# Moving the last maxima, a norm and a projection within the passes of a fused attention and expert block

## The chip, the core and the metric

The kernel runs on one core of a Trainium2 chip. The metric is the device time of one execution in microseconds, the median of several. Times of single instructions come from one profiled execution. TensorE has two clock levels, 1.2 and 2.4 GHz; "granted clock" is the mean level of a stretch as a share of the higher one.

## The reference

The input x has 64 sequences of 128 tokens with 128 features, the context 64 sequences of 120 tokens with 96 features. Both attentions have 16 heads of 8 features.

```
x = x + tanh(g_xattn) * cross_attention(layernorm(x), ctx, Wq.. bo)
x = x + tanh(g_ffn) * ffn(layernorm(x), ...)

ffn(x):
  h = rms(x, n1_w); q, k = rms per head of h@wq.T, h@wk.T; v = h@wv.T
  x = x + causal_attention(q, k, v) @ wo.T          (first 32 columns of it set to 0)
  xf = rms(x, n2_w)
  wts = top 2 of 4 of softmax(xf @ gate_w.T), normalised
  moe = wts0 * gelu(xf@e0_up)@e0_down + wts1 * (silu(xf@e1_w1) * (xf@e1_w2))@e1_down
      + wts2 * gelu(gelu(gelu(xf@e2_l1)@e2_l2)@e2_l3)@e2_l4
      + wts3 * gelu(gelu(xf@e3_down)@e3_up)@e3_out
  return x + moe                                    (first 32 columns of moe set to 0)
```

The layer norm of the second block and the rms norm inside it are nested: with v the variance and r = (v + 1e-5)^-1/2, h is (x - mean) * r * (r * r * v + 1.19e-7)^-1/2.

## The kernel before

**Groups and parts.** The 64 sequences go in 16 groups of 4. Five parts work on a group one after the other: N (layer norm, transposes, q, k and v of cross-attention), A (cross-attention), B (inputs of self-attention), D (self-attention, expert inputs and gates), M (the rest of the experts and the store). They are pipelined over groups: in step t, N works on group t + 1, A on t, B on t - 1, D on t - 2, M on t - 3. Steps -1 to 2 are the ramp, with fewer parts, steps 3 to 14 are a hardware loop of twelve passes, steps 15 to 18 the tail.

**Order.** Nothing is scheduled automatically. `SCHEDULE` is a list of works written by hand (`self_attention`, `second_experts`, `cross_attention`, `first_experts`), and every engine walks through the same list and issues its share of each work, in order. Ramp and tail steps take either the works of their parts from `SCHEDULE` or a list of their own (`second_group`, `third_group`, `last_self_values`). Engines wait for each other by semaphores: `filled` and `drained` of each PSUM bank, and named ones.

**Banks.** A work that writes PSUM takes the next bank of its ring: "w" has four (w0 to w3), "s2" and "f" are two names of the two banks s2a and s2b, "pv" and "t" have one each. PE may fill a bank when its previous use is drained.

**The scores of a sequence.** `estimate` computes rough scores of one sequence, in four works "s1", one per four heads, all issued together in four w banks (a quad). DVE takes their negative row maxima into mpad (L888, four TENSOR_REDUCE of 128x512 or 128x480). When the fourth sequence is done, "mT" transposes mpad on PE (L1098), ACT copies it to mT (L747), and SP issues four small DMAs that write it as extra rows into the stack of queries qd (L528, the semaphore m_loaded). `exact` computes the exact scores with these rows (L1110), which begin with waits for m_loaded and stacks_loaded; ACT takes their exponentials into probs (L766), POOL masks the causal ones. `values` multiplies by V, which ACT copies from the work "v". "oT", "nT" and "wo" normalise and project pairs of sequences.

**Nested norms.** After the second "wo" of A, DVE computes the statistics of x1 (L782 to L790). POOL makes, in six operations with two powers, the factors rB (L630 to L640): rB[0] is r for x2, rB[5] is the product for the input of self-attention. "A norm" on DVE applies the latter and writes hb; "hT" transposes hb on PE at the start of the next pass.

**Others.** "N stats" and "N norm" are the layer norm of the next group: DVE, one power on POOL (rsA, L608), and DVE again (xn, L819). "D out" writes yb, "D squares" is a square on POOL, a sum and a tiny operation on DVE, and leads to the power rM on POOL for "D norm". "gates 0" to "gates 3" are thirteen tiny DVE operations in four pieces. `queries_or_keys` copies q or k twice on ACT (L694, L699), `low_part` makes the remainder on DVE (L797, split_q and split_k) and drains the bank, `block_diagonal_keys` makes kd (L805).

## Time and profile before

| | us |
|---|---|
| median of 3 runs | 1191.6 |
| lowest and highest | 1188.81, 1195.52 |
| profiled execution, device time | 1192.36 |
| profiled execution, span of the core | 1190.6 |

| engine | busy us | share |
|---|---|---|
| PE (TensorE, matmuls) | 1038.0 | 87% |
| DVE (VectorE) | 792.6 | 67% |
| ACT (ScalarE) | 735.7 | 62% |
| POOL (GpSimd) | 351.5 | 30% |

The mean granted clock of TensorE is 0.941. A timeline row gives the start in us, the duration, the engine, the line, the operation, what it writes and reads, the shapes and the count, and in brackets the idle time ahead of it with what ended that idleness. Rows of one line merge several instructions. A group of the page gives busy time and mean ns, and after the bar the idle time before and what ended most of it.

### The profile page before, as it was taken

The page shows a single profiled execution, that of the slowest core. Times are in us where ns is not written, and L with a number is a line of the kernel's source. Part 1 is how long each engine was busy: PE and PEld are TensorE (multiplying, and loading weights), DVE is VectorE, ACT ScalarE, POOL GpSimd, SP SyncE. Part 2 cuts the span into 40 slices and gives each one's busy share as a digit, 9 for nine tenths or more (in the row PEclk, how much of TensorE's full clock was granted, in tenths as well). Part 3 has the DMA queues.
Part 4 walks back from the last instruction along what each step waited for, and adds up shares of the span by engine and source line. Part 5 has one row for each costly group of instructions (what it writes and reads, how often), then busy time and mean ns, then how long its engine had stood idle before and what let it go on. Part 6 is the DMA issues. An engine that isn't in the chain of part 4 may idle for free.

```text
span 1190.6 us, 26283 instructions
## 1 busy us (share of the span) xinstructions
PE 1038.0 (87%) x8578; PEld 645.1 (54%) x8578; DVE 792.6 (67%) x2153; ACT 735.7 (62%) x1329; POOL 351.5 (30%) x522
## 2 busy tenths in 40 slices
PE   3647798999999998999999999999999898988797
PEld 1324455555555565555565665555565555555454
DVE  7266666767777767777767676767767676764523
ACT  1334566767576666767666766767666676756353
POOL 4611415133141414133141514224141513214030
PEclk8667789999999999999999999999999999999899
DMA  5144444433434444333344444334344443220300
GB/s 179 32 119 107 120 108 120 110 101 90 103 67 115 119 116 119 90 99 99 93 88 115 119 116 106 90 100 98 79 114 115 119 114 98 82 45 34 83 1 18
DMA packets 78693, 114.27 MB, mean 96 GB/s; under 512 B 9153, under 2 KB 41537, under 8 KB 78529
## 3 DMA queue, kind: packets, MB, share of 16 engines
q1 hardware_dynamic: 78368, 111.58, 37.2%
q10 hardware_dynamic: 288, 2.21, 0.5%
q8 instruction: 22, 0.36, 0.1%
q14 instruction: 15, 0.11, 0.0%
HBM read 58.97 MB, written 53.74 MB: 95 GB/s over the span
## 4 chain that ended last, share of the span: by engine, by line
PE 55%; issue 17%; DVE 15%; ACT 6%; POOL 3%; DMA 2%; SPq 2%; DVEq 0%; POOLq 0%; ACTq 0%
PE ps_w L1157 11%; PE ps_pv L1131 7%; PE ps_s2a L1110 7%; PE ps_s2b L1110 5%; DVE mpadB L888 4%; PE ps_w L1175 4%; PE ps_t L1016 3%; PE ps_w L1016 3%; PE ps_w L1060 3%; DMA qdB<-mTB 2%; SPq L528 2%; PE ps_w L1092 2%; ACT probs L766 2%; DVE mpadA L888 2%; PE ps_w L1030 2%
## 5 line engine op out<-in xcount | busy, mean ns | idle before, releaser
L766 ACT ACTIVATE probs<-ps_s2a 120x512 f32<-120x512 f32 (+1 forms) x256 | 152.9, 597 | 129.7 <-PE ps_s2a L1110 124.6
L888 DVE TENSOR_REDUCE mpadA<-ps_w 128x4 f32<-128x480 f32 x256 | 150.3, 652 | 50.6 <-PE ps_w L1092 50.6
L888 DVE TENSOR_REDUCE mpadB<-ps_w 128x4 f32<-128x512 f32 x256 | 158.8, 685 | 28.9 <-PE ps_w L1092 28.9
L1157 PE MATMUL ps_w<-W,hid 128*128 128x96 f32 x1024 | 142.4, 298 | 18.6 <-DVE split_q L797 16.0
L1157 PEld LDWEIGHTS ps_w<-W,hid 128*128 128x128 f32 x1024 | 134.9, 212 | 33.8 <-DVE split_q L797 20.8
L766 ACT ACTIVATE probs<-ps_s2b 120x512 f32<-120x512 f32 (+1 forms) x256 | 152.6, 596 | 0.2 <-PE ps_s2b L1110 0.2
L666 POOL TENSOR_SCALAR_AFFINE_SELECT probs<-probs 128x1024 f32<-128x1024 f32 x128 | 140.0, 1093 | 0.0
L630 POOL TENSOR_TENSOR rB<-veB,neg_half 128x4 f32<-128x4 f32 x16 | 16.1, 1008 | 394.4 <-DVE veB L790 394.4
L1110 PE MATMUL ps_s2a<-qdB,kstB 128*128 128x512 f32 x128 | 66.1, 517 | 38.9 <-DMA qdB<-mTB 32.5
L1175 PE MATMUL ps_w<-xfT,W 128*128 128x512 f32 x160 | 85.0, 620 | 0.0
L665 POOL TENSOR_TENSOR tick<-one 128x1 f32<-128x1 f32 x128 | 24.9, 195 | 186.9 <-ACT probs L766 183.1
L1168 PE MATMUL ps_s2a<-hid,W 128*128 128x512 f32 x160 | 79.2, 609 | 0.0
L917 DVE SCALAR_TENSOR_TENSOR ym<-ps_w,gates,ym 128x96 f32<-128x96 f32 x192 | 47.6, 311 | 47.1 <-PE ps_w L1157 47.1
L762 ACT ACTIVATE hid<-ps_s2a 128x512 f32<-128x512 f32 x80 | 47.8, 598 | 47.2 <-PE ps_s2a L1168 34.6
L1110 PE MATMUL ps_s2a<-qdA,kstA 128*120 128x512 f32 x128 | 65.5, 511 | 10.9 <-DMA qdA<-mTA 4.7
L770 ACT ACTIVATE oT<-ps_pv 128x512 f32<-128x512 f32 x64 | 38.2, 598 | 51.8 <-PE ps_pv L1131 51.5
L1131 PE MATMUL ps_pv<-probs,VA 120*18 120x128 f32 x2048 | 70.0, 278 | 0.0
L1131 PE MATMUL ps_pv<-probs,VB 128*18 128x128 f32 x2048 | 68.7, 274 | 0.1
L617 POOL TENSOR_TENSOR xf<-x 128x512 f32<-128x512 f32 x16 | 16.6, 1040 | 170.4 <-DVE yb L949 170.4
L1131 PEld LDWEIGHTS ps_pv<-probs,VA 120*18 120x18 f32 x2048 | 51.3, 99 | 24.1 <-issue 23.4
L1110 PEld LDWEIGHTS ps_s2a<-qdB,kstB 128*128 128x128 f32 x128 | 24.8, 194 | 70.3 <-issue 56.8
L1131 PEld LDWEIGHTS ps_pv<-probs,VB 128*18 128x18 f32 x2048 | 50.4, 97 | 18.5 <-issue 17.7
(176 smaller groups left out, 2096.3 us busy)
## 6 DMA issues: line engine op xcount, KB each, us to landing
scratch_Aq<-split_q SPq DMA_DIRECT2D x48, 256.0 KB, 2.4
qdA<-scratch_Aq SPq DMA_DIRECT2D x64, 192.0 KB
scratch_Bq<-split_q SPq DMA_DIRECT2D x48, 256.0 KB, 2.4
scratch_Bk<-split_k SPq DMA_DIRECT2D x48, 256.0 KB, 3.0
qdB<-scratch_Bq SPq DMA_DIRECT2D x64, 192.0 KB
kstB<-scratch_Bk SPq DMA_DIRECT2D x64, 192.0 KB
scratch_Ak<-split_k SPq DMA_DIRECT2D x48, 240.0 KB, 2.9
kstA<-scratch_Ak SPq DMA_DIRECT2D x64, 180.0 KB
```

Of the source, the lines that this page charges most:

```text
L666: pool.affine_select(out=tile, in_=tile, compare_op=ALU.is_ge, fill=0.0, base=0, pattern=[[0, 2 * HT], [1, P]], channel_multiplier=-1).the ...
L762: nc.scalar.activation(hid[:, HID_AT[index[0]] + index[1], :], bank[:], ACT.Gelu).then_inc(done, 1)
L766: nc.scalar.activation(probs[0:k, slot_of(part, *index), :], bank[0:k, :], ACT.Exp, scale=SCALE if part == "A" else 1.0).then_inc(done, 1)
L770: nc.scalar.activation(oT[:], bank[:], ACT.Copy).then_inc(done, 1)
L888: nc.vector.tensor_reduce(mneg[OP[part]][:, :, c, b], bank[:, 0:HT * k].rearrange("p (h k) -> p h k", h=HT), AX.X, ALU.max, negate=True).t ...
L917: ins = nc.vector.scalar_tensor_tensor(out=ym[:, b, KEEP:P], in0=bank[:, b * UP:(b + 1) * UP], scalar=gates[:, b, e:e + 1], in1=y[:, b, KE ...
L1016: ins = nc.tensor.transpose(psum[st.bank[key]][:, b * P:(b + 1) * P], of(b), identf[:])
L1110: mm(o, kst[p][:, c, b * k:(b + 1) * k], qd[p][:, :, c, b * P:(b + 1) * P], start=True, stop=True).then_inc(done, 1)
L1131: ins = mm(psum[st.bank[last]][32 * j:32 * j + VS, at:at + P], VB[p][0:k, first:first + VS], probs[0:k, slot_of(part, b, c), j * P:(j + 1) ...
L1157: ins = mm(bank[:, b * UP:(b + 1) * UP], hid[:, HID_AT[h] + k, b * P:(b + 1) * P], w[f"down{index[1]}"][:, k * UP:(k + 1) * UP], start=k = ...
L1168: ins = mm(bank[:], w[name][:, k * HID + c * P:k * HID + (c + 1) * P], hid[:, HID_AT[h] + k, :], start=k == 0, stop=k == chunks[-1])
L1175: mm(bank[:], w[name][:, c * P:(c + 1) * P], xfT[:], start=True, stop=True).then_inc(done, 1)
```

## The change

Five edits, all but one moves in the lists. (1) In `first_experts`, estimate B 3 goes from behind "wo" 1 of A, its statistics and the base of the next group, to behind "nT" 1; "mT" of B goes ahead of q and v; the second pair of silu fills (e1_w1 and e1_w2, index 1) goes from ring w to ring f; gates 1 goes ahead of q, gates 2 ahead of "A norm", v and k. (2) In `second_experts`, "N norm" goes ahead of "wo" 1 and "out" of D, and "D squares" behind qT and kT. (3) In `cross_attention`, the projection v of B goes behind the first pair of exact scores. (4) The factor of the nested norms becomes one power of (v * (1 + RMS_EPS) + RMS_EPS * LN_EPS), which DVE computes as vrB beside veB; POOL has two operations instead of six, and x2's initial value now waits for b_pow. (5) In ramp and tail steps ("st.parts != PARTS") SP issues two of the four maxima DMAs and ACT the other two, and the diagonal keys of N are made ahead of the low part of k. `third_group` and `last_self_values` are changed alike.

```
-            + one("D", "out", 0, None) + one("D", "squares", 0, None) + one("N", "norm", 0, None) + one("B", "qT") + one("B", "kT")
+            + one("D", "out", 0, None) + one("B", "qT") + one("B", "kT") + one("D", "squares", 0, None)
...
-    return (one("B", "v") + exact("A", 0, 0) + down(2) + exact("A", 0, 2) + one("N", "xT")
+    return (exact("A", 0, 0) + one("B", "v") + down(2) + exact("A", 0, 2) + one("N", "xT")
...
-                        for j in range(HT):
+                        for j in range(HT if st.parts == PARTS else HT // 2):
...
+                        pool.tensor_tensor(rB[:, 1], vrB[:], neg_half[:], ALU.pow).then_inc(b_rs, 1)
                         pool.tensor_tensor(rB[:, 0], veB[:], neg_half[:], ALU.pow).then_inc(b_pow, 1)
-                        pool.wait_ge(b_pow, g * 5 + 1)
-                        pool.tensor_tensor(rB[:, 1], rB[:, 0], rB[:, 0], ALU.mult).then_inc(b_pow, 1)
-                        pool.wait_ge(b_pow, g * 5 + 2)
-                        pool.tensor_tensor(rB[:, 2], rB[:, 1], mvB[:, :, 1], ALU.mult).then_inc(b_pow, 1)
-                        pool.wait_ge(b_pow, g * 5 + 3)
-                        pool.tensor_tensor(rB[:, 3], rB[:, 2], rms_eps[:], ALU.add).then_inc(b_pow, 1)
-                        pool.wait_ge(b_pow, g * 5 + 4)
-                        pool.tensor_tensor(rB[:, 4], rB[:, 3], neg_half[:], ALU.pow).then_inc(b_pow, 1)
-                        pool.wait_ge(b_pow, g * 5 + 5)
-                        pool.tensor_tensor(rB[:, 5], rB[:, 4], rB[:, 0], ALU.mult).then_inc(b_rs, 1)
...
+                        if st.parts != PARTS:
+                            act.wait_ge(done, st.fills(*key))
+                            for j in range(HT // 2, HT):
...
+                if both is not None:
+                    nc.vector.tensor_scalar(both[:], mv[:, :, 1], 1.0 + RMS_EPS, RMS_EPS * LN_EPS, ALU.mult, ALU.add).then_inc(stats, 1)
...
+                        if work == "k" and st.parts != PARTS:
+                            block_diagonal_keys(part, "A", g)
```

The three places below are taken from step 2 of the ramp, which walks through the same list as a pass of the loop, only without part M, and so without its rows.

The first is PE's end of a step, from the second silu fill to the transpose of the maxima or the projections of the next group. Line 1175 is a fill of experts from xfT, 1016 "nT", 1088 and 1092 the estimate with the causal rows, 1144 "wo", 1030, 1040 and 1034 q, v and k, 1098 "mT". Before:

```order
L1175 MATMUL ps_w<-xfT,W 128x512
L1016 MATMUL ps_t<-identf,on 128x128 x2
L1175 MATMUL ps_s2b<-xfT,W 128x512
L1144 MATMUL ps_t<-W,onT 128x128 x2
L1088 MATMUL ps_w<-causal_k,causal_q 128x512 x4
L1092 MATMUL ps_w<-kdB,qTbB 128x512 x4
L1175 MATMUL ps_s2a<-xfT,W 128x512
L1175 MATMUL ps_s2b<-xfT,W 128x512
L1030 MATMUL ps_w<-xnT,W 128x512
L1040 MATMUL ps_w<-W,ctT 120x128 x4
L1098 MATMUL ps_w<-identf,mpadB 128x128
```

The same place in the changed kernel, whose lines are numbered five higher here:

```order
L1180 MATMUL ps_s2a<-xfT,W 128x512
L1021 MATMUL ps_t<-identf,on 128x128 x2
L1093 MATMUL ps_w<-causal_k,causal_q 128x512 x4
L1097 MATMUL ps_w<-kdB,qTbB 128x512 x4
L1180 MATMUL ps_s2b<-xfT,W 128x512
L1149 MATMUL ps_t<-W,onT 128x128 x2
L1180 MATMUL ps_s2a<-xfT,W 128x512
L1180 MATMUL ps_s2b<-xfT,W 128x512
L1103 MATMUL ps_w<-identf,mpadB 128x128
L1035 MATMUL ps_w<-xnT,W 128x512
L1045 MATMUL ps_w<-W,ctT 120x128 x4
```

The estimate has moved ahead of one fill and "wo", the transpose of the maxima ahead of q and v, and the silu fill is in an s2 bank.

The second is DVE at the same place, from x1 or the maxima on. Line 937 is x1, 782 to 790 the statistics, 888 the maxima, 797 the low part, 973 to 975 gates 1, 834 hb. Before:

```order
L937 SCALAR_TENSOR_TENSOR x<-ps_t,tg,xb 128x256
L782 BN_STATS stB<-x 128x6 x4
L785 MEMSET sm 128x1
L787 BN_AGGR mvB<-stB 128x2 x4
L790 TENSOR_SCALAR veB<-mvB 128x4
L888 TENSOR_REDUCE mpadB<-ps_w 128x4 x4
L797 SCALAR_TENSOR_TENSOR split_q<-ps_w,vc,split_q 128x512
L973 TENSOR_REDUCE sm<-lg 128x4
L974 RECIPROCAL sm<-sm 128x4
L975 TENSOR_TENSOR lg<-lg,sm 128x16
L834 TENSOR_SCALAR hb<-x,mvB,rB 128x128 x4
L797 SCALAR_TENSOR_TENSOR split_k<-ps_w,vc,split_k 128x480
```

In the changed kernel:

```order
L893 TENSOR_REDUCE mpadB<-ps_w 128x4 x4
L942 SCALAR_TENSOR_TENSOR x<-ps_t,tg,xb 128x256
L781 BN_STATS stB<-x 128x6 x4
L784 MEMSET sm 128x1
L786 BN_AGGR mvB<-stB 128x2 x4
L790 TENSOR_SCALAR vrB<-mvB 128x4
L791 TENSOR_SCALAR veB<-mvB 128x4
L978 TENSOR_REDUCE sm<-lg 128x4
L979 RECIPROCAL sm<-sm 128x4
L980 TENSOR_TENSOR lg<-lg,sm 128x16
L798 SCALAR_TENSOR_TENSOR split_q<-ps_w,vc,split_q 128x512
L984 TENSOR_TENSOR cmp<-lg 128x4x3
```

The maxima have moved ahead of x1 and the statistics, gates 1 ahead of split_q; behind the last row come seven more of gates 2 and only then hb.

The third is DVE between the statistics of the next group and the diagonal keys of B. Line 942 is "wo" 1 of D, 949 "out", 847 and 849 "squares", 819 "N norm". Before:

```order
L942 TENSOR_TENSOR x<-ps_t,x 128x2x96
L949 SCALAR_TENSOR_TENSOR yb<-x,tg,xc 128x512
L847 TENSOR_REDUCE ssM<-xf 128x4
L849 TENSOR_SCALAR msM<-ssM 128x4
L819 TENSOR_SCALAR xn<-xt,mvA,rsA 128x128 x4
L797 SCALAR_TENSOR_TENSOR split_q<-ps_w,qns,split_q 128x512
L797 SCALAR_TENSOR_TENSOR split_k<-ps_w,vc,split_k 128x512
```

In the changed kernel:

```order
L820 TENSOR_SCALAR xn<-xt,mvA,rsA 128x128 x4
L947 TENSOR_TENSOR x<-ps_t,x 128x2x96
L954 SCALAR_TENSOR_TENSOR yb<-x,tg,xc 128x512
L798 SCALAR_TENSOR_TENSOR split_q<-ps_w,qns,split_q 128x512
L798 SCALAR_TENSOR_TENSOR split_k<-ps_w,vc,split_k 128x512
L806 TENSOR_SCALAR kdB<-kTbB,pick 128x512 x4
L849 TENSOR_REDUCE ssM<-xf 128x4
L851 TENSOR_SCALAR msM<-ssM 128x4
```

The norm is now ahead of "wo" and "out", the sum of squares behind the diagonal keys.

## Rows read from the trace of the kernel before

**Rows 1.** Stretches: us, busy PE, PEld, DVE, ACT, POOL, clock, DMA share, GB/s.
```profile
526.82:593.18 66.36, 61.52 (x537) 37.98 (x537) 48.65 (x137) 45.73 (x83) 20.16 (x29) 1.00 0.42 105
593.18:661.06 67.88, 63.03 (x536) 39.67 (x537) 48.65 (x137) 45.85 (x83) 20.16 (x29) 0.97 0.41 103
593.80:597.30 3.50, 3.50 (x19) 3.50 (x18) 0.83 (x5) 1.68 (x3) 1.60 (x3) 0.53 0.94 340
626.00:628.00 2.00, 0.71 (x7) 0.67 (x7) 2.00 (x6) 1.97 (x3) 1.51 (x2) 1.00 0.00 0
```

**Rows 2.** The page's costliest groups: down projection; first bank of exact scores.
```profile
L1157 PE MATMUL ps_w<-W,hid 128*128 128x96 f32 x1024 | 142.4, 298 | 18.6 <-DVE split_q L797 16.0
...
L1110 PE MATMUL ps_s2a<-qdB,kstB 128*128 128x512 f32 x128 | 66.1, 517 | 38.9 <-DMA qdB<-mTB 32.5
```

**Rows 3.** Timeline of PE at the end of one pass and the next's start.
```profile
649.67 0.44 PE L1016 MATMUL ps_t<-identf,on 128*128 128x128 f32 x2
...
654.12 1.12 PE L1030 MATMUL ps_w<-xnT,W 128*128 128x512 f32 x2 [0.25 <-DVE mpadB L888]
...
661.06 0.49 PE L1110 MATMUL ps_s2a<-qdB,kstB 128*128 128x512 f32 x1 [2.22 <-DMA qdB<-mTB]
...
668.39 0.38 PE L1092 MATMUL ps_w<-kdA,qTbA 32*128 32x480 bf16 x4
```

**Rows 4.** Timelines of DVE, ACT and POOL over the same seam.
```profile
651.98 0.87 DVE L782 BATCH_NORM_STATS2 stB<-x 128x6 f32<-128x128 f32 x4
...
653.38 2.48 DVE L888 TENSOR_REDUCE mpadB<-ps_w 128x4 f32<-128x512 f32 x4
656.58 0.75 DVE L797 SCALAR_TENSOR_TENSOR split_q<-ps_w,vc,split_q 128x512 fp32r<-128x512 f32 x1 [0.72 <-ACT split_q L699]
...
658.08 1.12 DVE L834 TENSOR_SCALAR hb<-x,mvB,rB 128x128 f32<-128x128 f32 x4
...
660.75 0.18 DVE L979 TENSOR_TENSOR cmp<-lg 128x12 f32<-128x12 f32 x1
...
661.79 0.17 DVE L985 TENSOR_REDUCE sm<-lg 128x4 f32<-128x16 f32 x1
...
655.28 0.69 ACT L694 ACTIVATE qTbA<-ps_w,vc 128x512 bf16<-128x512 f32 x1 [0.77 <-PE ps_w L1030]
...
656.97 0.26 ACT L747 ACTIVATE mTB<-ps_w 64x128 fp32r<-64x128 f32 x1
...
659.49 1.28 ACT L766 ACT_TABLE_LOAD   x1
...
653.55 1.01 POOL L630 TENSOR_TENSOR rB<-veB,neg_half 128x4 f32<-128x4 f32 x1 [26.04 <-DVE veB L790]
...
656.74 1.27 POOL L649 TENSOR_TENSOR xb<-xt,gxbo 128x512 f32<-128x512 f32 x1
```

**Rows 5.** Timelines of PE, DVE, POOL and ACT at the start of cross-attention.
```profile
627.33 2.02 PE L1157 MATMUL ps_w<-W,hid 128*128 128x96 f32 x16 [1.29 <-DVE split_q L797]
...
625.50 1.12 DVE L819 TENSOR_SCALAR xn<-xt,mvA,rsA 128x128 f32<-128x128 f32 x4
626.53 0.75 DVE L797 SCALAR_TENSOR_TENSOR split_q<-ps_w,qns,split_q 128x512 fp32r<-128x512 f32 x1
...
624.45 1.02 POOL L608 TENSOR_TENSOR rsA<-veA,neg_half 128x4 f32<-128x4 f32 x1
...
626.30 1.28 ACT L766 ACT_TABLE_LOAD   x1
627.59 0.60 ACT L766 ACTIVATE probs<-ps_s2a 120x512 f32<-120x512 f32 x1
```

**Rows 6.** Timeline of PE in ramp steps 0 and 1 and tail step 15.
```profile
37.70 0.75 PE L1110 MATMUL ps_s2a<-qdA,kstA 128*120 128x512 f32 x1 [4.71 <-DMA qdA<-mTA]
...
125.35 0.77 PE L1110 MATMUL ps_s2a<-qdB,kstB 128*128 128x512 f32 x1 [2.81 <-issue]
...
1060.95 0.33 PE L1098 MATMUL ps_w<-identf,mpadB 128*128 128x128 f32 x1 [2.04 <-DVE mpadB L888]
```

More of the change, by code:

```diff
@@ L147, in first_experts @@
     return (fill("D", "e1_w1", 0, "w") + one("A", "wo", 0, "t") + fill("D", "e1_w2", 0, "w") + values("A", 3)
-            + one("D", "gates", 0, None) + fill("D", "e1_w1", 1, "w") + one("A", "oT", 1, "t") + fill("D", "e1_w2", 1, "w")
-            + one("A", "nT", 1, "t") + fill("D", "e2_l1", 0) + one("A", "wo", 1, "t") + one("A", "stats", 0, None)
-            + one("N", "base", 0, None) + estimate("B", 3) + fill("D", "e2_l1", 1) + fill("D", "e3_down", 0) + one("N", "q")
-            + one("D", "gates", 1, None) + one("A", "norm", 0, None) + one("N", "v") + one("B", "mT") + one("N", "k")
-            + fill("D", "e0_up", 0) + one("D", "gates", 2, None) + fill("D", "e0_up", 1, "w") + one("D", "gates", 3, None))
+            + one("D", "gates", 0, None) + fill("D", "e1_w1", 1) + one("A", "oT", 1, "t") + fill("D", "e1_w2", 1)
+            + one("A", "nT", 1, "t") + estimate("B", 3) + fill("D", "e2_l1", 0) + one("A", "wo", 1, "t") + one("A", "stats", 0, None)
+            + one("N", "base", 0, None) + fill("D", "e2_l1", 1) + fill("D", "e3_down", 0) + one("D", "gates", 1, None)
+            + one("B", "mT") + one("N", "q") + one("D", "gates", 2, None) + one("A", "norm", 0, None) + one("N", "v") + one("N", "k")
+            + fill("D", "e0_up", 0) + fill("D", "e0_up", 1, "w") + one("D", "gates", 3, None))
 def slot_of(part, b, c):
@@ L160, with of_parts @@
 SCHEDULE = self_attention() + second_experts() + cross_attention() + first_experts()
+def of_parts(parts, order=None):
+    return [use for use in order or SCHEDULE if use[0] in parts]
 def first_group():
@@ L192, in third_group @@
             + one("B", "init", 0, None) + one("B", "copy", 0, None) + values("A", 0)
-            + exact("A", 2, 0) + one("N", "xT") + exact("A", 2, 2) + values("A", 1)
-            + exact("A", 3, 0) + one("A", "oT", 0, "t") + estimate("B", 1) + exact("A", 3, 2) + values("A", 2)
-            + one("A", "nT", 0, "t") + one("A", "wo", 0, "t") + values("A", 3) + estimate("B", 2)
+            + exact("A", 2, 0) + estimate("B", 1) + exact("A", 2, 2) + one("N", "xT") + values("A", 1)
+            + exact("A", 3, 0) + one("A", "oT", 0, "t") + estimate("B", 2) + exact("A", 3, 2) + values("A", 2)
+            + one("A", "nT", 0, "t") + one("A", "wo", 0, "t") + values("A", 3) + estimate("B", 3)
             + one("A", "oT", 1, "t") + one("A", "nT", 1, "t") + one("A", "wo", 1, "t")
-            + one("A", "stats", 0, None) + one("N", "base", 0, None) + estimate("B", 3)
-            + one("N", "q") + one("A", "norm", 0, None) + one("N", "v") + one("B", "mT") + one("N", "k"))
+            + one("A", "stats", 0, None) + one("N", "base", 0, None) + one("B", "mT")
+            + one("N", "q") + one("N", "v") + one("A", "norm", 0, None) + one("N", "k"))
 def last_self_values():
@@ L210, in last_self_values @@
             + fill("D", "e1_w1", 0, "w") + fill("D", "e1_w2", 0, "w") + one("D", "gates", 0, None)
-            + fill("D", "e1_w1", 1, "w") + fill("D", "e1_w2", 1, "w") + fill("D", "e2_l1", 0) + one("D", "gates", 1, None)
+            + fill("D", "e1_w1", 1) + fill("D", "e1_w2", 1) + fill("D", "e2_l1", 0) + one("D", "gates", 1, None)
             + fill("D", "e2_l1", 1) + fill("D", "e3_down", 0) + one("D", "gates", 2, None)
@@ L245, in uses_before @@
     return n
-def of_parts(parts):
-    return [use for use in SCHEDULE if use[0] in parts]
 PARTS = "NABDM"
@@ L402, in build @@
         rsA = sb("rsA", [P, G])
-        rB = sb("rB", [P, 6, G])
+        rB = sb("rB", [P, 2, G])
+        vrB = sb("vrB", [P, G])
         hs, hr = sb("hs", [P, 2 * H * G]), sb("hr", [P, 2 * H * G])
@@ L778, in _, with statistics @@
         def _(dve):
-            def statistics(src, stats_of, mv, ve, stats, g):
+            def statistics(src, stats_of, mv, ve, stats, g, both=None):
+                n = g * (4 if both is not None else 3)
                 for b in range(G):
@@ L829, in step @@
                             dve.wait_ge(drained[b], n)
-                        statistics(x1, stB, mvB, veB, b_stats, g)
+                        statistics(x1, stB, mvB, veB, b_stats, g, both=vrB)
                     elif (part, work) == ("A", "norm"):
@@ L837, in step @@
                     elif (part, work) == ("B", "init"):
+                        dve.wait_ge(b_pow, g + 1)
                         if not st.first("B"):
```

18 lines of the change are left out of this document (11 added, 7 removed).

## The prediction

> **What bounds the kernel now.** I read the page's costliest groups first, for what TensorE (PE) waits for, then PE's timeline, then those of VectorE (DVE), ScalarE (ACT) and GpSimd (POOL) at the two waits found. PE is the bound: of a loop pass of 66.36 us it is busy for 61.52 [rows 1]. A pass is one trip of the twelve-trip loop; self-attention of group g starts each with the first exact scores of part D. Two waits stand out in the groups: 32.5 us before these first scores, for the DMA of the row maxima (qdB<-mTB), and 16.0 us before a down projection, for DVE's split_q [rows 2].
>
> The first wait is 2.22 us in the pass shown [rows 3]; 13 seams between passes (the ramp's last step ahead of them) have it alike. It costs more than its length. A pass without a fallen clock lasts 66.36 us, one with it 67.88; in the latter the granted clock is about half (0.53, so mostly 1.2 of the 2.4 GHz) for the 3.5 us right after the wait [rows 1]. I counted 11 such falls behind the 13 waits. The second wait, 1.29 us, is not followed by one: the clock across it is 1.00 [rows 1, 5]. So a fall costs 67.88 - 66.36 = 1.5 us, and only the long wait brings it.
>
> **Seam between two passes, before.** From the transposes of the second normalised pair (nT, 649.67) to the first estimate of the next pass (668.39) PE takes 18.72 us [rows 3]: 0.25 waiting for DVE's maxima before q, 2.22 for the DMA, 1.5 for the clock, the rest work. The maxima of the fourth quad start on DVE at 653.38 only, because x1 and its statistics stand ahead (from 651.98) [rows 4]. Their transpose then waits behind q and v, ACT copies it at 656.97 [rows 4], and from there to the first scores it is 661.06 - 656.97 = 4.09 us: the copy, four issues on SP's queue, the landing.
>
> **Seam, after.** PE runs nT, then the estimate. Its four banks are free by then, since the second silu pair has gone from ring w to ring f. DVE ends the silu product at about 651.0 (x1, 0.5 us, stands between it and 651.98 with 0.4 of idleness), takes the four maxima in the 2.48 us of its row, until 653.5, then x1 (0.5), statistics with one more tiny operation (1.5 + 0.17), until 655.6. PE meanwhile does e2_l1, wo, e2_l1 and e3_down: the same steps that lay between nT and q before, whose 654.12 less the 0.25 of wait is 653.87, so it reaches the maxima transpose at about 653.8, with the maxima just done. ACT has the gelu of e3_down ahead of the copy, which I place at 654.45. Plus 4.09 the maxima have landed at 658.55. PE has the same steps before it as from 654.12 to 658.84 (661.06 less 2.22), 4.7 us, and is there at about 658.5: a wait under 0.1 instead of 2.22.
>
> Behind that three things come close. (1) hb: POOL's first power takes 1.01 us [rows 4], so b_rs stands at 656.7, in place of a chain of six that took 3.2 us until the next POOL operation began. One power alone is enough to keep POOL off the path, but DVE now has gates 1 (0.8: from split_q's end, 656.58 + 0.67, to hb at 658.08) and gates 2 (660.75 to 661.79, 1.04) ahead of hb [rows 4]. Its line is split_q 656.4 to 657.1, gates 2 to 658.15, hb to 659.2; PE wants hb at 659.0. Wait 0.2. (2) The drain of k by DVE, 0.7 later, against the down projection at 659.8: 0.1. (3) ACT: from q's first copy to the end of its table load is a closed row of work, 655.28 to 660.77 before; it ends at 660.55 after, while PE comes 2.5 us earlier. Exponentials, hT, exponentials, four copies of qk then end at 664.95, and the estimate, which needs all four banks, starts at 665.05 where PE was ready at 664.7: 0.35. So the seam ends at 665.05 - 649.67 = 15.4 instead of 18.7: 3.34 saved where the clock fell, 1.84 where it did not. 13 x 1.84 + 11 x 1.5 = 40.4 us.
>
> A rule of the Trainium skill speaks against (3). ScalarE: Activation LUTs (What ACT_TABLE_LOAD costs) says that a switch costs a load of 1283 ns and a drain of about 1380 ns. The trace has the load alone: it starts at 626.30 behind a copy and takes 1.28, and the exponential follows at 627.59, 0.01 us later [rows 5]. By the page the start of D would be 1.4 us later in 13 passes, 18 us less gain; I go by the rows.
>
> **Start of cross-attention.** Before: PE does v, then the first pair of scores, until about 626.0, and waits 1.29 us until 627.33 because DVE's split_q runs at 626.53 only; ahead of it stands the norm of the next group (xn, 625.50, 1.12 us), which waits for POOL's power at 624.45, itself queued behind POOL's square of x2 [rows 5]. After: the power is first on POOL, right behind the statistics, and xn (1.12) fills a stretch in which DVE stood idle before wo; wo and out follow, and split_q comes some 1.6 us earlier, at about 624.9, so that the bank is free before PE wants it at 625.9. The square, its sum and the power rM come some 2 us later; what they feed on ACT stands four pairs of exponentials further on and has that slack. The wait goes: 1.3. Moving v behind the first pair brings the pair forward by v's 0.85 us, towards the landing of its own maxima, of which I put the margin at 0.5. ACT's copy of v now stands between two pairs of exponentials (0.6 us, as long as each of them [rows 5]), and PE then has to wait about 0.2 for a bank. Net 1.1, in 12 passes: 13.2 us. Ends for this edit: 0 (another wait takes its place) to 1.3.
>
> **Ramp and tail.** Here the maxima are issued half by SP, half by ACT. Four issues take 2.4 us, so up to 1.2 us each time; the exposed places are the wait of 4.71 [rows 6] and about four more. The third ramp step gets its maxima ahead of q, v, k: 2.81 of wait there [rows 6]. In the first tail step the maxima's 2.04 [rows 6] mostly go. Diagonal keys ahead of the low part save 0.7 twice and delay one store by 1.1. The trace of before shows no maxima issued by ACT: an issue could cost ACT nothing or 0.6 us each, as on SP. I bound all of it by 0 and 14 us and take 8. The Trainium skill (DMA: Bandwidth & Descriptors, Issuing engines are not separate DMA queues) says that two issuers save only the time of initiating; no run here shows yet what they save.
>
> **Sum.** 40.4 + 13.2 + 8 = 61.6 us saved. Four places of the seam are ties within 0.3 us in my line, and ties in a chain of three engines add up one way: I take off 0.3 per pass, 4 us. 57.6 from the profiled execution's 1192.4 (span 1190.6) gives 1134.8, so 1135. The profiled execution is 0.8 above the median of 1191.6; I leave that in.
>
> **Rivals.**
> (a) The clock still falls behind the seam, because hb, k and the banks bring several short waits in place of one. For it: they sum to 0.75 us within 7 us. Against: 1.29 us in one piece kept the clock at 1.00. It gives back 16.5: 1151.
> (b) DVE becomes the bound of the seam: hb comes 1 us later than in my line, say since the silu product or the maxima start later. For it: DVE has one gap alone, of 0.72, between 651.98 and 658.08 [rows 4]. It gives 13 us back: 1148.
> (c) Slower than before: the same mechanism pushed to its end. The maxima (2.5), gates 1 and gates 2 (1.8) all moved ahead of hb, 4.3 us of DVE work. If none of it found a gap, hb would be ready at 663.5 instead of 659.2, PE would stand 4.5 us at the hb transposes and the clock would fall each time: first estimate at about 670.4, 2.0 later than 668.39, against 1.1 gained in cross-attention: 0.9 x 13 = 12 us lost, less the few us of ramp and tail, 1198. It decides from about 3 us of wait at hb. Against: DVE waited 0.72 us for ACT before split_q [rows 4], a gap that gates 1 fills, and so the chain needs only a part of the 4.3.
> (d) The reordering moves waits without removing them (the copy of the maxima sits in ACT behind a late gelu, the first scores wait for their maxima): within 6 us of before, 1189.
>
> **Chances.** Forecast 0.72; (a) 0.11; (b) 0.09; (d) 0.04; (c) 0.04. Faster than before by over 0.5% (what a measurement of this kernel tells from no change): 0.92; within 0.5% 0.04; slower 0.04. Range: 1119 (ramp and tail at 14, ties at nothing, and a few us for waits in the cold ramp that a faster clock would shorten) to 1158 (beyond a and b, and short of d and c).
>
> **What would show it.** The group of first scores on qdB has under 5 us of wait for the DMA instead of 32.5; the down projection's wait for split_q is gone; the clock of a pass reads 1.00; passes last 63 to 64 us; the hb transposes show a new wait of 0.1 to 0.4 and the first estimate one for ACT's qk. Wrong would be: hb transposes waiting over 1 us, a clock under 0.99 in the passes, or exponentials of the second cross-attention pair holding PE for more than 0.5.

## The result, and the profile after

The changed kernel takes 1139.9 us (median of 4 runs, 1139.5 to 1140.6) against 1192.2 for the kernel before beside it (4 runs, 1188.8 to 1195.5): a ratio of 0.956, 95% interval 0.953 to 0.959. The forecast was 1135 with a range of 1119 to 1158. The profiled execution has a span of 1138.1 us, 52.5 less than before.

Two passes of the loop after, in the view of stretches (us, busy PE, PEld, DVE, ACT, POOL, clock, DMA share, GB/s), which answer to the two passes of [rows 1] (each stretch starts 0.23 us ahead of part D's first scores):

```profile
500.52:564.82 64.30, 61.68 (x537) 38.04 (x536) 49.97 (x136) 45.37 (x84) 19.32 (x26) 1.00 0.43 108
564.82:629.12 64.30, 61.67 (x537) 38.04 (x536) 49.97 (x136) 45.38 (x84) 19.33 (x26) 1.00 0.43 108
```

Eleven of the loop's twelve passes now last 64.3 at a clock of 1.00, where they lasted 66.36 or 67.88. The first, straight behind the ramp, lasts 66.4 with a fallen clock. TensorE's idle time in a pass fell from 4.84 to 2.62 (length less busy). VectorE is 1.32 us busier (49.97 against 48.65) although the change adds it a single 0.17 us operation. The two stretched operations shown below add 1.77, and one that was stretched before got 0.2 shorter; they lead to what was forecast wrongly.

The page's groups that answer to [rows 2], and that of the new statistics power (busy, mean ns of one | idle time before them, and what ended it):

```profile
L1162 PE MATMUL ps_w<-W,hid 128*128 128x96 f32 x1024 | 129.8, 281 | 4.4 <-ACT probs L764 1.1
...
L631 POOL TENSOR_TENSOR rB<-vrB,neg_half 128x4 f32<-128x4 f32 x16 | 16.1, 1007 | 372.4 <-DVE veB L791 372.4
...
L1115 PE MATMUL ps_s2a<-qdB,kstB 128*128 128x512 f32 x128 | 64.9, 507 | 10.5 <-DMA qdB<-mTB 5.6
```

The wait of the first scores for their maxima went from 32.5 to 5.6 us in all, that of the down projection for split_q from 16.0 to nothing in the list. The down matmuls' mean fell from 298 to 281 ns without a change to them: 28 of the 1024 run at the lower clock, where 153 did.

TensorE's timeline of the seam after, which answers to [rows 3]:

```profile
556.23 0.44 PE L1021 MATMUL ps_t<-identf,on 128*128 128x128 f32 x2
...
560.27 0.27 PE L1103 MATMUL ps_w<-identf,mpadB 128*128 128x128 f32 x1
...
565.05 0.49 PE L1115 MATMUL ps_s2a<-qdB,kstB 128*128 128x512 f32 x1 [0.20 <-DMA qdB<-mTB]
...
566.59 0.65 PE L1021 MATMUL ps_w<-identf,hb 128*128 128x128 f32 x4 [0.81 <-DVE hb L835]
567.33 2.00 PE L1162 MATMUL ps_w<-W,hid 128*128 128x96 f32 x16
...
571.46 0.70 PE L1065 MATMUL ps_w<-W,hT 128*128 128x256 f32 x2 [0.35 <-DVE ym L922]
...
572.72 0.38 PE L1097 MATMUL ps_w<-kdA,qTbA 32*128 32x480 bf16 x4
```

From the second nT transposes to the first scores it is 8.82 us (565.05 - 556.23), and to the first estimate 16.49. The maxima now wait 0.20 where they waited 2.22. In their place stand two new waits, both for VectorE: 0.81 for hb, and 0.35 for ym, which holds the bank that the fourth query-key product needs. (In the experiments, "a pass" is the length of one undisturbed trip of the loop.)

What VectorE and GpSimd do over that seam (the answer to [rows 4]):

```profile
562.78 0.75 DVE L798 SCALAR_TENSOR_TENSOR split_q<-ps_w,vc,split_q 128x512 fp32r<-128x512 f32 x1 [0.32 <-ACT split_q L691]
...
564.04 0.20 DVE L987 TENSOR_REDUCE lg<-cmp 128x16 f32<-128x48 f32 x1
564.27 1.03 DVE L988 SCALAR_TENSOR_TENSOR lg<-lg 128x16 f32<-128x16 f32 x1
565.34 1.12 DVE L835 TENSOR_SCALAR hb<-x,mvB,rB 128x128 f32<-128x128 f32 x4
...
568.01 0.17 DVE L990 TENSOR_REDUCE sm<-lg 128x4 f32<-128x16 f32 x1
568.22 1.08 DVE L991 TENSOR_SCALAR sm<-sm 128x4 f32<-128x4 f32 x1
569.33 0.18 DVE L992 RECIPROCAL sm<-sm 128x4 f32<-128x4 f32 x1
```

```profile
562.06 1.01 POOL L631 TENSOR_TENSOR rB<-vrB,neg_half 128x4 f32<-128x4 f32 x1 [24.44 <-DVE veB L791]
563.03 1.01 POOL L632 TENSOR_TENSOR rB<-veB,neg_half 128x4 f32<-128x4 f32 x1
564.01 1.27 POOL L641 TENSOR_TENSOR xb<-xt,gxbo 128x512 f32<-128x512 f32 x1
...
568.18 1.09 POOL L658 TENSOR_SCALAR_AFFINE_SELECT probs<-probs 128x1024 f32<-128x1024 f32 x1
569.24 0.40 POOL L665 TENSOR_TENSOR ym<-yb,one 128x128 f32<-128x128 f32 x1
```

Read the two lists beside each other. L988 works on 16 numbers per partition and takes 0.17 us where nothing disturbs it. Here it takes 1.03 and ends at 565.30, just when GpSimd's 128x512 addition ends (565.28). L991 takes 1.08 and ends at 569.30, with the mask (569.27). Over the whole kernel L988 is long in 12 of 16 cases and L991 in 12 of 16, each time beside such a GpSimd operation, and 0.17 in the others. VectorE's operations stand in the forecast order; 0.86 and 0.91 us come on top because of what runs on GpSimd beside them.

The trace of the kernel before had the sign of it already, in a row that the prediction did not show:

```profile
657.66 0.39 DVE L975 TENSOR_TENSOR lg<-lg,sm 128x16 f32<-128x16 f32 x1
```

L975, the last operation of gate stage 1, also takes 0.17 where nothing disturbs it. In 13 of 16 cases it took 0.36 to 0.50 and ended 0.03 behind the end of the same addition, which ran from 656.74 for 1.27 us [rows 4].

The start of cross-attention, which answers to [rows 5]:

```profile
594.00 1.11 DVE L820 TENSOR_SCALAR xn<-xt,mvA,rsA 128x128 f32<-128x128 f32 x4 [1.14 <-POOL rsA L609]
...
596.17 0.74 DVE L798 SCALAR_TENSOR_TENSOR split_q<-ps_w,qns,split_q 128x512 fp32r<-128x512 f32 x1
```

```profile
596.35 0.78 PE L1115 MATMUL ps_s2a<-qdA,kstA 128*120 128x512 f32 x1
596.96 0.40 PE L1115 MATMUL ps_s2b<-qdA,kstA 128*120 128x512 f32 x1
597.20 1.05 PE L1070 MATMUL ps_w<-W,hT 128*128 128x128 f32 x8
598.09 1.92 PE L1162 MATMUL ps_w<-W,hid 128*128 128x96 f32 x16
```

xn fills an idle stretch of VectorE, split_q is done at 596.91, and the down projection at 598.09 waits for nothing.

The 52.5 us come from these places (starts of part D compared between the two traces): 37.9 in the loop's twelve passes (811.7 to 773.8 in all), 10.5 before them (first start of D 125.35 to 116.93, the ramp's last stretch 62.2 to 60.1), 4.1 behind. From the transpose of A's maxima to the first estimate of B a pass went from 11.77 to 10.45 us, so 1.32 belongs there, 15.8 in twelve; the other 22 belong to the seam.

### The profile page after: what moved, and what is told of

Read it like the earlier page. It is cut to its first block, busy times and chain, and to the rows that moved or that the text cites. A ratio compares the mean times of both kernels' runs of the same rounds, so it can differ in the third digit from the quotient of the medians.

```text
span 1138.1 us, 26049 instructions
## 1 busy us (share of the span) xinstructions
PE 1018.1 (89%) x8578; PEld 625.7 (55%) x8578; DVE 809.2 (71%) x2169; ACT 729.4 (64%) x1329; POOL 338.1 (30%) x458
## 4 chain that ended last, share of the span: by engine, by line
PE 56%; DVE 24%; ACT 10%; issue 7%; DMA 1%; ACTq 1%; POOL 1%; DVEq 0%; SPq 0%; POOLq 0%
PE ps_pv L1136 9%; PE ps_w L1162 7%; PE ps_s2a L1115 5%; PE ps_s2a L1173 5%; DVE mpadA L893 4%; PE ps_s2b L1115 4%; PE ps_s2b L1180 4%; PE ps_t L1021 4%; DVE mpadB L893 3%; ACT probs L764 3%; PE ps_t L1149 3%; PE ps_w L1180 3%; PE ps_w L1097 2%; DVE ym L922 2%; PE ps_w L1093 2%
## 5 line engine op out<-in xcount | busy, mean ns | idle before, releaser
L658 POOL TENSOR_SCALAR_AFFINE_SELECT probs<-probs 128x1024 f32<-128x1024 f32 x128 | 139.8, 1092 | 0.0
L1162 PE MATMUL ps_w<-W,hid 128*128 128x96 f32 x1024 | 129.8, 281 | 4.4 <-ACT probs L764 1.1
L1162 PEld LDWEIGHTS ps_w<-W,hid 128*128 128x128 f32 x1024 | 122.1, 195 | 16.4 <-issue 13.4
L631 POOL TENSOR_TENSOR rB<-vrB,neg_half 128x4 f32<-128x4 f32 x16 | 16.1, 1007 | 372.4 <-DVE veB L791 372.4
L1115 PE MATMUL ps_s2a<-qdA,kstA 128*120 128x512 f32 x128 | 68.3, 534 | 11.6 <-DMA qdA<-mTA 6.1
L1115 PE MATMUL ps_s2a<-qdB,kstB 128*128 128x512 f32 x128 | 64.9, 507 | 10.5 <-DMA qdB<-mTB 5.6
L771 ACT ACTIVATE onT<-ps_t 128x256 f32<-128x256 f32 x64 | 24.5, 383 | 57.3 <-PE ps_t L1021 57.3
L1115 PE MATMUL ps_s2b<-qdA,kstA 128*120 128x512 f32 x128 | 58.9, 460 | 0.0
L1149 PEld LDWEIGHTS ps_t<-W,onT 128*128 128x128 f32 x256 | 39.3, 197 | 31.6 <-issue 20.6
```

The costliest lines, as they stand in the source:

```text
L658: pool.affine_select(out=tile, in_=tile, compare_op=ALU.is_ge, fill=0.0, base=0, pattern=[[0, 2 * HT], [1, P]], channel_multiplier=-1).the ...
L1115: mm(o, kst[p][:, c, b * k:(b + 1) * k], qd[p][:, :, c, b * P:(b + 1) * P], start=True, stop=True).then_inc(done, 1)
L1149: ins = mm(bank[:, s * n:(s + 1) * n], onT[:, s * P:(s + 1) * P], w["Wo"] if part == "A" else w["wo"], start=True, stop=True)
L1162: ins = mm(bank[:, b * UP:(b + 1) * UP], hid[:, HID_AT[h] + k, b * P:(b + 1) * P], w[f"down{index[1]}"][:, k * UP:(k + 1) * UP], start=k = ...
```

## The experiments

The forecast held, but its seam was 1.1 us short in each pass. Theory A (contention): two small vector operations are held by GpSimd's wide ones, and that is why hb and ym are late. Rival B: VectorE simply has too much in front of hb (gate stages 1 and 2). Theory C: the fall of the clock behind the 2.2 us wait was worth 1.5 us a pass by itself. The diffs below are shortened; names and lists are abridged.

**1. GpSimd's wide addition made narrow.** In the loop xb = x + bias covers 8 of 512 columns; the rest of xb is left out, so the part of the result that uses it is not the reference's.

```diff
-pool.tensor_tensor(xb[:], xt[:], bias, ALU.add)
+pool.tensor_tensor(xb[:, 0, 0:8], xt[:, 0, 0:8], gxbo[:, 0:8], ALU.add)
```

> The changed kernel, but in the loop's passes POOL's sum xb = xt + bias covers 8 of its 512 columns only (part of the result is left out, for a look at time alone). It tells what holds hb back at the seam. In the changed kernel the tiny DVE operation at L988 takes 1.03 us instead of 0.18, just while POOL's xb (1.27 us) runs. Theory, contention of DVE with POOL's wide operation: L988 falls to about 0.2, hb starts 0.85 earlier, the 0.80 us wait of PE before the hb transposes falls under 0.2, and a pass lasts 63.5 instead of 64.30: 1130. Rival, DVE's own queue is simply that long: L988 stays near 1.0 and the pass at 64.3: 1140.

Measured: 1130.7 us (2 runs; ratio to before 0.950), a pass of 63.67, L988 back at 0.17 us, no wait at hb, 0.6 at the fourth query-key product instead of 0.35. 64.30 - 63.67 = 0.63 us a pass was the price of the addition's place. Theory A holds for hb. About a quarter of the 0.81 that hb gives back is taken by the next wait, and that one is no longer the stretch's: L991 is back at 0.17 too, and ym waits 1.77 for GpSimd's copy of yb into it.

**2. Gate stage 2 behind the diagonal keys.** All work is kept, hb has less in front of it.

```diff
-one("B","mT") + one("N","q") + one("D","gates",2,None) + one("A","norm",0,None) + one("N","v") + one("N","k")
-  + fill("D","e0_up",0)
+one("B","mT") + one("N","q") + one("A","norm",0,None) + one("N","v") + one("N","k")
+  + fill("D","e0_up",0) + one("D","gates",2,None)
```

> The changed kernel with gates 2 back behind the diagonal keys, so that hb follows split_q at once. If the 1.04 us of gates 2 (or its stretched 1.9) is what delays hb, hb is ready about 0.9 to 1.9 earlier, the 0.80 wait before the hb transposes goes, passes last 63.5 and the time is about 1130. By the contention theory hb itself now falls into POOL's xb: its four operations stretch until about 0.1 behind xb's end, hb is ready about 0.3 earlier at most, and gates 2 and 3, now last, delay the first gated sum of the down projection: passes of 64.2 to 64.6, 1139 to 1144.

Measured: 1138.0 us (4 runs, 1134.2 to 1139.3; ratio to before 0.956, 0.955 to 0.958), a pass of 64.33 (one of the twelve lasted 65.68 at a clock of 0.97): no gain. hb comes earlier and TensorE no longer waits for it, but now hb itself runs into the addition. DVE's row, then POOL's:

```profile
557.25 2.16 DVE L835 TENSOR_SCALAR hb<-x,mvB,rB 128x128 f32<-128x128 f32 x4
```
```profile
557.80 1.27 POOL L641 TENSOR_TENSOR xb<-xt,gxbo 128x512 f32<-128x512 f32 x1
```

The four operations take 2.16 instead of 1.12, and the gates behind them are late for ym: the fourth product waits 1.19. With less in front of hb the pass stays the same, since the collision moves with the order. This alone does not rule out rival B, because the late gates take back what hb gives. Experiments 1 and 5 do: there VectorE has gate stages 1 and 2 in front of hb, and the wait at hb is gone.

**3. Six GpSimd operations for the factor again**, in the order of the changed kernel.

```diff
-pool.tensor_tensor(rB[:, 1], vrB[:], neg_half[:], ALU.pow).then_inc(b_rs, 1)
-pool.tensor_tensor(rB[:, 0], veB[:], neg_half[:], ALU.pow).then_inc(b_pow, 1)
+... pow, mult, mult, add, pow, mult, as in the kernel before
```

> The changed kernel with the factor of the nested norms made in six POOL operations again. My prediction held one power enough to keep POOL off the path: then hb waits for b_rs, which comes 3.2 instead of 1.0 us behind veB, at about the time hb starts now (565.3 in the pass that starts at 565.05), so hb is at most 0.1 later; and as POOL's xb then runs 1.2 later, gates 2 is not stretched. Expected 64.2 to 64.6 per pass, within 0.4% of the changed kernel. Rival: the one power is worth its 2.2 us less on POOL at the seam: passes of 65 to 66.5, 1150 to 1165.

Measured: 1168.0 us (2 runs; ratio 0.981), passes of 65.3 to 67.8. My expectation was wrong; the rival (1150 to 1165) was near, and short by 3: in this order the single power is worth 28 us (1168.0 less 1139.9). VectorE and GpSimd at that place:

```profile
643.28 1.99 DVE L844 TENSOR_SCALAR hb<-x,mvB,rB 128x128 f32<-128x128 f32 x4 [0.93 <-POOL rB L641]
```
```profile
642.97 0.20 POOL L641 TENSOR_TENSOR rB<-rB 128x4 f32<-128x4 f32 x1
643.14 1.27 POOL L650 TENSOR_TENSOR xb<-xt,gxbo 128x512 f32<-128x512 f32 x1
```

hb waits 0.93 for the chain's end, and then its own run is stretched by the addition that starts in the same moment. TensorE waits 1.8 us at hb, and 7 of the loop's 12 passes read a clock of 0.95 or 0.97. One pass of either kind:

```profile
442.98:510.76 67.78, 64.64 (x537) 40.82 (x536) 50.11 (x135) 45.86 (x84) 20.46 (x30) 0.95 0.41 103
...
577.02:642.34 65.32, 61.68 (x537) 38.05 (x536) 50.11 (x135) 45.54 (x84) 20.46 (x30) 1.00 0.43 107
```

**4. The kernel before with two matmuls in the wait.** Two 128x512 products whose result nobody reads are added ahead of part D's first scores, so that TensorE is not idle there; nothing is left out.

```diff
 if index == (0, 0):
+    for _ in range(2): mm(psum["t"][:], w["Wq"], xnT[:], start=True, stop=True)
     pe.wait_ge(stacks_loaded[p], ...)
```

> The kernel before with two useless matmuls (128x512, about 0.9 us each) put on PE ahead of its wait for the maxima at the head of each loop pass; nothing else moves, and the wait for the DMA ends when it did. It separates the clock from the wait. Theory, the clock falls because PE stands idle there: PE is idle for 0.4 instead of 2.2 us, the clock reads 1.00 in all passes, every pass lasts 66.36 instead of 67.88 in 11 of 13: 1176, 16 us less, although no wait is shorter. Rival, the fall has to do with the work behind the seam: clock and time stay, 1192.

Measured: 1175.5 us (2 runs; ratio 0.987), eleven loop passes at 66.4 and all twelve at a clock of 1.00 (the last, whose next start lies in the tail without the added matmuls, lasts 67.0), as theory C had it to 1 us:

```profile
517.23:583.60 66.37, 63.25 (x540) 38.76 (x540) 48.64 (x136) 45.72 (x83) 20.17 (x29) 1.00 0.42 105
```

TensorE is 1.7 us busier than in the clean pass of [rows 1] and the pass is not longer. The falls were worth 15 us against the kernel before beside it (1190.7), shown: ten passes at 1.5.

**5. The addition ahead of the powers.** It now runs beside the statistics of x1. All work is kept.

```diff
-one("A","wo",1,"t") + one("A","stats",0,None) + one("N","base",0,None)
+one("A","wo",1,"t") + one("N","base",0,None) + one("A","stats",0,None)
```

> The changed kernel with POOL's xb ahead of the two powers, all work kept. POOL stands idle when the second wo has drained (560.4 in the pass that starts at 565.05) until 562.06, and the DVE operations of that stretch are statistics, none of which I have seen stretched. Contention theory: xb ends before gates 2 and hb, nothing of the seam is stretched but L991, hb is ready 0.85 earlier, the pass is that of the run with the small xb, 63.67, the time 1131. Rival: the powers, now 0.2 to 0.4 later behind xb, hold hb as long as the stretched operation did: pass 64.1 to 64.3, 1137 to 1140.

Measured: **1129.6 us** (4 runs, 1128.3 to 1131.6; ratio to before 0.949, 0.947 to 0.951), a pass of 63.66 and no wait at hb: the gain of experiment 1 with the whole work. What is left at the head of the pass is DVE's ym, and it waits for GpSimd:

```profile
564.28 0.99 DVE L922 SCALAR_TENSOR_TENSOR ym<-ps_w,gates,yb 128x96 f32<-128x96 f32 x4 [1.77 <-POOL ym L665]
```

**6. The same with gate stages 1 and 2 earlier** (stage 1 ahead of the second oT, stage 2 ahead of q's low part).

```diff
-fill("D","e1_w1",1) + one("A","oT",1,"t")
+fill("D","e1_w1",1) + one("D","gates",1,None) + one("A","oT",1,"t")
-one("D","gates",1,None) + one("B","mT") + one("N","q") + one("D","gates",2,None)
+one("D","gates",2,None) + one("B","mT") + one("N","q")
```

> The same, and gates 1 ahead of the second oT, where DVE idles about 1 us, and gates 2 ahead of q's low part, where it idles 0.3. DVE reaches hb about 0.6 earlier still and gates 3 ends at about 567.1, before POOL's first mask at about 567.9, so that L991 isn't stretched either and the gated sum no longer holds the bank of the fourth qk (0.35 of wait now, 0.6 with the small xb). From D's first scores to the first estimate 6.1 to 6.3 us instead of 7.67: passes of 62.7 to 62.9, time 1119 to 1122. Rival: ACT is the next bound of the seam (table load, two pairs of exponentials, hT, four copies): 6.5 or more, passes of 63.2, 1126. If gates 1 in its new place delays the normalising behind oT, the gain shrinks by what PE waits before nT, at most 0.6 a pass.

Measured: 1129.8 us (4 runs, 1128.2 to 1130.4), no gain over experiment 5. A miss: I took the gates for ym's releaser. DVE's ym still waits, now 2.54 us, for GpSimd's copy of yb into ym, which stands in GpSimd's queue behind the pass's first causal mask, and that waits for ScalarE's exponentials.

**7. That copy ahead of the mask**, with experiment 5's order (first kernel) and with 6's (second). In steps without part D the copy stays where it was.

```diff
+elif D's scores (0, 1):  wait y_ready, stored; copy yb -> ym columns 0:KEEP
     ... mask ...
-elif M's first down projection:  the same waits and copy
```

> The kernel after with GpSimd's x+bias ahead of the two powers and, besides, its copy of the first output columns (ym <- yb, 0.40) issued ahead of the pass's first causal mask instead of behind it. Before this the accumulation into ym at the head of the pass waited 1.77 for that copy, and the fourth query-key matmul pair 0.58 for ym. Theory (that copy's place in GpSimd's queue is what holds the matmuls once the base is early): the 0.58 goes, start to estimates 7.02 -> 6.4, pass 63.66 -> 63.1, median 1129.6 - 13 x 0.58 = 1122. Rival (the accumulation is held by the down matmuls or by its gates anyway): within 0.3% of 1129.6.

> As the kernel with the early base and the copy ahead of the first mask, and with gate stages 1 and 2 one place earlier as well. There the fourth query-key pair waited 0.75 behind a 2.54 wait of the accumulation for the copy. Theory: start to estimates 7.04 -> 6.3, pass 63.74 -> 63.0, median 1129.8 - 13 x 0.75 = 1120. Rival (vector work of the gates stretched by GpSimd, or the first masks, take it): within 0.3% of 1129.8.

Measured: 1118.9 us (4 runs, 1116.9 to 1121.2; ratio 0.940, 0.938 to 0.942) and **1114.3 us** (4 runs, 1113.6 to 1117.2; ratio to before 0.937, 0.935 to 0.939), passes of 62.84 and 62.72. Both are below what was expected. The copy's place was the bound, and a little more than the waits came free: start of D to first estimate went from 7.02 to 6.19 and from 7.04 to 6.01. TensorE's timeline in the faster one, to be read against the seam above:

```profile
552.24 0.49 PE L1121 MATMUL ps_s2a<-qdB,kstB 128*128 128x512 f32 x1 [0.20 <-DMA qdB<-mTB]
552.57 0.40 PE L1121 MATMUL ps_s2b<-qdB,kstB 128*128 128x512 f32 x1
552.80 0.60 PE L1027 MATMUL ps_w<-identf,hb 128*128 128x128 f32 x4
553.24 1.92 PE L1168 MATMUL ps_w<-W,hid 128*128 128x96 f32 x16
...
555.71 2.00 PE L1071 MATMUL ps_w<-W,hT 128*128 128x256 f32 x8
...
558.27 0.38 PE L1103 MATMUL ps_w<-kdA,qTbA 32*128 32x480 bf16 x4
```

hb and the eight query-key matmuls run without a gap; this kernel is about 2% faster than the changed one (0.937 against 0.956 of the kernel before).

**8. Only the cross-attention part of the change, and everything but it.** The first is the kernel before with the norm, the squares and the value projection moved. The second is the changed kernel with these three put back.

```diff
-fill("M","e2_l3",0) + one("D","wo",1,"t") + one("D","out",0,None) + one("D","squares",0,None) + one("N","norm",0,None)
+fill("M","e2_l3",0) + one("N","norm",0,None) + one("D","wo",1,"t") + one("D","out",0,None)
   + one("B","qT") + one("B","kT")
+  + one("D","squares",0,None)
-one("B","v") + exact("A",0,0) + down(2)
+exact("A",0,0) + one("B","v") + down(2)
```

> The kernel before with the two edits at the start of cross-attention alone (norm of the next group ahead of wo and out of D, squares behind kT, v behind the first pair). By my account of the change they take 1.3 us of wait out of each of 12 passes and nothing else: from the maxima transpose of A to the first estimate of B 10.45 instead of 11.77, the seam as before with its 2.2 us wait and clock falls, 1192 - 12 x 1.3 = 1176, up to 5 either way for where the falls land. Rival: without the earlier seam the gain is given back at the wait for the maxima's DMA (its time being fixed by something else than PE): 1190.

> The kernel after with the order of the cross-attention's start as it was before (N norm and D squares in their old places, value projection ahead of the first exact pair). What is left of the change is the seam with the one power, and ramp and tail. The two parts are additive in a pass (seam 16.49 instead of 18.72; mT to the second quad of estimates 11.77 instead of 10.45): pass 64.30 + 1.32 = 65.6, no clock falls in the passes, median 1139.9 + 13 x 1.3 = 1157. Rival (the waits overlap or the clock falls again at the 1.3 wait): pass over 66.3, over 1168; or the slack takes it, under 1150.

Measured: cross-attention alone 1164.3 us (2 runs, 1159.4 and 1169.1; ratio 0.979, 0.971 to 0.986); without it 1153.9 (2 runs, 1151.8 and 1156.0; ratio 0.969, 0.967 to 0.972). In the pass the parts add up: 65.65 without, 64.30 with it, 1.35 against the 1.32 read from the milestones. In the whole they do not (27 + 37 is more than 52), and the expectation for the first kernel, 1176 within 5, missed by 12. In the traces its twelve passes save 19.4 us and those of the second 23.8, together 43.2 against 37.9 for the whole change. Of the 5.3 too many, 3.0 are two clock falls fewer than before behind the 2.2 us wait, and 2.0 are the first pass, which lasts 65.76 without a fall in the second kernel and 66.41 with one in the changed kernel, where it should be 1.35 shorter. The rest lies in the ramp, whose length varies from run to run, and the first kernel's two runs are 10 us apart. Two passes of the first kernel:

```profile
380.45:445.45 65.00, 61.38 (x536) 38.13 (x536) 48.51 (x135) 45.46 (x84) 20.17 (x29) 1.00 0.43 107
445.45:511.97 66.52, 62.89 (x536) 39.70 (x536) 48.52 (x135) 45.68 (x84) 20.16 (x29) 0.97 0.42 105
```

Four of the loop's 12 passes are of the first kind, where before only 2 were clean. The seam's wait is the same 2.2 us in both kinds, so its length alone does not decide whether the clock falls. The clean ones come every third pass here; before, the two (526.82 and 796.79) are four passes apart, and there is none four passes ahead of the first. Passes with the same work fall or don't, so the work of a pass alone does not decide it; I did not settle what does.

**9. The value projection ahead of the first pair again** (the last two lines of the diff above, undone in the changed kernel).

> The changed kernel with the projection v of B back ahead of the first pair of exact scores. PE's work between the maxima transpose of A and the first estimate of B is 10.48 us either way and the change runs it in 10.45 without a wait, so if the norm's move alone frees split_q in time the place of v is worth nothing: 64.3 per pass, 1140. Rival, v hides the time in which the first pair's exponentials wait for their table load: without it the second pair waits 0.5 to 0.9: 64.8 to 65.2, 1146 to 1151.

Measured: 1141.7 us (2 runs, 1141.5 and 1141.9), a pass of 64.79. TensorE waits for the exponentials, once a pass:

```profile
599.20 0.49 PE L1115 MATMUL ps_s2a<-qdA,kstA 128*120 128x512 f32 x1 [0.45 <-ACT probs L764]
```

The rival was right about the pass: v's matmuls behind the pair cover the table load of ScalarE, 0.49 us a pass. The medians differ by 1.8 only, less than 12 x 0.49 = 5.9. The profiled run's first start of D came 2.5 earlier (114.39 against 116.93; over the runs of the changed kernel and its variants it lies between 114.0 and 117.5), and its first pass had no clock fall (64.86 against 66.41). I take the pass, not the median, as the measure.

**10. The maxima's copies at ramp and tail all issued by SyncE again.**

> The kernel after with all four copies of the estimates' maxima issued by SyncE again at ramp and tail, instead of two by ScalarE. My sum put 1.5 to 2.5 on this split over the five steps. Theory: the transfers' own time dominates (waits at the heads of ramp steps were 5.72 and 1.42 with the split, 4.71 and 2.39 without), so the median is within 0.2% of 1139.9. Rival (two issuers halve the wait): 1142 to 1145.

Measured: 1141.8 us (4 runs, 1135.9 to 1148.3), which the time does not tell from 1139.9. The trace does, at single places. From the transpose of the maxima to the first scores of ramp step 1 it is 88.42 - 84.81 = 3.61 us with two issuers and 86.78 - 82.19 = 4.59 with one (4.58 before); step 2 and the two tail steps show the same 1.0 us (3.60 against 4.58, 3.77 against 4.75, 3.56 against 4.53). In step 0, where the prediction saw the largest wait, nothing can be told: 6.19 against 6.48, while the variants with two issuers lie between 5.95 and 6.46 and the kernel before at 5.19. And at the end of ramp step 2 the split costs: issuing two copies takes ScalarE 1.41 us, its next copies and activation are late, and the first scores of the loop wait 1.34 instead of 0.24. Changed kernel first, then this one:

```profile
172.16 1.41 ACTq L744 DMA_DIRECT2D qdB<-mTB  x2
...
177.06 0.50 PE L1115 MATMUL ps_s2a<-qdB,kstB 128*128 128x512 f32 x1 [1.34 <-ACT hid L760]
```
```profile
171.35 0.50 PE L1109 MATMUL ps_s2a<-qdB,kstB 128*128 128x512 f32 x1 [0.24 <-DMA qdB<-mTB]
```

From nT to these scores it is 9.91 us with the split and 8.81 without. So the split saves 1.0 us at each of four places and costs 1.1 at a fifth, about 2.8 in all. TensorE's rows of ramp step 1, with two issuers and with one:

```profile
84.81 0.48 PE L1103 MATMUL ps_w<-identf,mpadA 128*128 128x128 f32 x1 [3.70 <-DVE mpadA L893]
88.42 0.75 PE L1115 MATMUL ps_s2a<-qdA,kstA 128*120 128x512 f32 x1 [1.42 <-issue]
```
```profile
82.19 0.47 PE L1097 MATMUL ps_w<-identf,mpadA 128*128 128x128 f32 x1 [3.71 <-DVE mpadA L887]
86.78 0.75 PE L1109 MATMUL ps_s2a<-qdA,kstA 128*120 128x512 f32 x1 [2.40 <-issue]
```

## Why the prediction was right, and where it was off

**nT to first scores.** Forecast 8.88 us with a wait under 0.1, measured 8.82 with 0.20. Right step by step: the maxima's transpose starts 4.04 us behind nT (forecast 4.1).

**The clock.** It was to read 1.00 in the passes and does in eleven of twelve. In those rival (a), several short waits that make the clock fall, is out (0.20, 0.81 and 0.35 us in the pass shown). The first pass fell as (a) describes: its head has waits of 1.34, 0.45 and 1.10 us, the first from the split issue (experiment 10), and the clock fell behind them (in experiment 10 it fell behind 0.24, 0.72 and 1.10 too). That a fall costs 1.5 us is shown by experiment 4.

**First scores to first estimate.** This is the step that failed: the forecast put 0.2 for hb, 0.1 for k's drain and 0.35 for ACT's banks, 6.5 us in all; measured 7.67. hb waited 0.8, and the 0.35 came from ym on VectorE, not from ScalarE. I had counted gate stage 2 as in the kernel before (1.04 us) and moved it to where GpSimd's addition runs; the trace of before gave its duration only where it stood alone. The 0.8 for gate stage 1 was read from rows that hold L975's stretch of 0.2, and went unnoticed. The seam is 16.49 long, not 15.4: rival (b) named VectorE as the next bound with the wrong reason for it (a late silu product or late maxima), and hb came about 0.6 later than forecast where (b) had 1. Experiments 1 and 5 show the real reason. In the sum the seam gave not 40.4 less 4 for ties, but about 22 in twelve seams and some 2 in the thirteenth (18.7 less 16.49 = 2.2 where the clock fell, 0.7 where it did not).

**One power instead of six operations.** I called one power "enough to keep POOL off the path" and gave it no term. By experiment 3 it is worth 28 us, more than the seam's own gain in the sum: without it hb comes 0.9 later for the chain and 0.9 more for the stretch, and the clock falls again. Rival (c) had the mechanism, a wait at hb followed by a fall, but put the point at which it decides at 3 us of wait; experiment 3 has falls at 1.8, though it still ends faster than before.

**Start of cross-attention.** Forecast 1.1 a pass, measured 1.32 (trace) and 1.35 (experiment 8), since no bank held TensorE behind v. 15.8 us against 13.2.

**ScalarE's table load.** Forecast without a drain. After the change ACT's load starts at 565.50, takes 1.28, and the exponential follows at 566.80, as in [rows 5]. The drain of about 1380 ns that the Trainium skill, ScalarE: Activation LUTs (What ACT_TABLE_LOAD costs), adds to a load does not appear, neither here nor there.

**Ramp and tail.** Forecast 8 within 0 to 14. What is left of the 52.5 behind the loop's seams and cross-attention is 12.4, of which the split issue explains about 2.8. It gave nothing at the wait of 4.71 that the prediction named first (5.72 after), and an issue cost ScalarE 0.7 us, against "nothing or 0.6". The rest is the reordered ramp steps and luck with the clock, which I did not take apart.

**The sum.** 57.6 forecast, 52.3 by the medians. The seam was 12 us too good, cross-attention 2.6 and ramp and tail 4.4 too poor; the errors partly cancel, so that the total is better than its terms is partly luck.

## What to carry to other kernels

When you move small vector operations, look at what GpSimd runs at their new place, not only at what VectorE has in front of them: a duration read where GpSimd was idle isn't the duration beside its wide operations. When a chain on a side engine feeds a value that the bounding engine waits for, price the chain by the wait and by the clock behind it; and once a wait is gone, follow what its operation was queued behind (here a copy behind a mask behind exponentials), since moving that one copy gave as much again as the contention had.
